# Two mixture-of-experts stages that take each slot's rows by gather and give its sums back by scatter, in a four-stage kernel

## The reference

```python
x = x + tanh(g_xattn[0]) * L0_xattn(ctx_1024, layernorm(x), ...)        # stage a
x = x + tanh(g_ffn[0])   * L0_ffn(layernorm(x), router_w, router_b, w1, w3, w2)   # stage f: 4 experts, top 2
x = x + tanh(g_xattn[1]) * L1_xattn(layernorm(x), ctx_1024, ...)        # stage g
x = x + tanh(g_ffn[1])   * L1_ffn(layernorm(x), Wg, W1, W2, W3)         # stage m: 8 experts, top 2
# an expert: y = (silu(t @ w1) * (t @ w3)) @ w2, hidden width 2048 (f) or 1024 (m)
# out = sum over the token's two experts of gate * y
```

## Time and profile before

| what | us |
|---|---|
| median of 3 runs (2413.39 to 2417.11) | 2416.28 |
| the profiled execution's own time | 2416.51 |
| its span | 2414.3 |
| TensorE busy | 1988.6 (82%) |
| TensorE weight loads busy | 1595.4 (66%) |
| VectorE busy | 1078.6 (45%) |
| ScalarE busy | 855.8 (35%) |
| GpSimd busy | 569.1 (24%) |
| stage f, 1141.7 to 1762.2 | 620.5 |
| stage g, 1762.2 to 1914.7 | 152.5 |
| stage m, 1914.7 to 2414.3 | 499.6 |

### The profile page before, as it was taken

The page is one execution under the profiler, slowest core; times in us unless marked ns, Lnnn a source line. Parts: engine busy times, 40 slices in busy tenths (PEclk is TensorE's granted clock), DMA queues, the critical chain, the costliest instruction groups (busy, mean ns, idle before and its releaser), DMA issues. The chain is left out here.

```text
span 2414.3 us, 35504 instructions
## 1 busy us (share of the span) xinstructions
PE 1988.6 (82%) x12312; PEld 1595.4 (66%) x12312; DVE 1078.6 (45%) x2301; ACT 855.8 (35%) x1799; POOL 569.1 (24%) x522
## 2 busy tenths in 40 slices
PE   3899999999999999996289999999737628888883
PEld 2577777777776777774177777777516427776772
DVE  4445454545445454433433333333254445445444
ACT  2333333433343433332333333333124234444440
POOL 2020202020202010000213333333130023445443
PEclk9999999999999999998589999999868859999896
DMA  6501010101000010000633333333560364434446
GB/s 213 182 35 47 8 39 15 40 9 34 21 32 23 10 45 8 15 8 17 217 114 100 100 100 104 103 101 99 203 215 1 110 229 138 121 122 145 133 122 179
DMA packets 114324, 214.75 MB, mean 89 GB/s; under 512 B 21584, under 2 KB 24432, under 8 KB 114188
## 3 DMA queue, kind: packets, MB, share of 16 engines
q1 hardware_dynamic: 104876, 186.02, 24.8%
q0 software_dynamic: 6144, 13.13, 1.9%
q10 hardware_dynamic: 3168, 13.89, 1.4%
HBM read 172.82 MB, written 40.17 MB: 88 GB/s over the span
## 5 line engine op out<-in xcount | busy, mean ns | idle before, releaser
L360 POOL TENSOR_TENSOR a_rows<-a_rows,a_gain_x 128x512 f32<-128x512 f32 (+1 forms) x48 | 66.2, 1379 | 773.1 <-DVE a_rows L680 773.1
L848 PE MATMUL f_banks<-f_wab_hi,f_x_hi 128*128 x448 | 185.9, 415 | 15.3 <-DVE f_wab_lo L1438 11.9
L488 PE MATMUL a_kv_ps<-a_kvin_hi,a_wk_hi 128*128 128x512 f32 (+1 forms) x512 | 196.5, 384 | 0.9 <-DVE a_kvin_lo L687 0.9
L488 PE MATMUL a_kv_ps<-a_wv_hi,a_kvin_hi 128*128 128x512 f32 (+1 forms) x448 | 185.9, 415 | 11.8 <-DVE a_k_lo L704 7.0
L848 PE MATMUL m_banks<-m_wab_hi,m_x_hi 128*128 x512 | 163.4, 319 | 31.7 <-DVE m_wab_lo L1438 28.6
L490 PE MATMUL a_kv_ps<-a_kvin_hi,a_wk_lo 128*128 128x512 f32 (+1 forms) x512 | 180.4, 352 | 0.0
L489 PE MATMUL a_kv_ps<-a_kvin_lo,a_wk_hi 128*128 128x512 f32 (+1 forms) x512 | 180.3, 352 | 0.0
L490 PE MATMUL a_kv_ps<-a_wv_hi,a_kvin_lo 128*128 128x512 f32 (+1 forms) x448 | 178.1, 397 | 0.0
L850 PE MATMUL f_banks<-f_wab_hi,f_x_lo 128*128 x448 | 177.8, 397 | 0.0
L489 PE MATMUL a_kv_ps<-a_wv_lo,a_kvin_hi 128*128 128x512 f32 (+1 forms) x448 | 177.6, 396 | 0.0
L849 PE MATMUL f_banks<-f_wab_lo,f_x_hi 128*128 x448 | 176.7, 394 | 0.0
(11 more groups left out here) (347 smaller groups left out, 4799.0 us busy)
## 6 DMA issues: line engine op xcount, KB each, us to landing
f_raw<-f_pieces SPq DMA_DIRECT2D x192, 256.0 KB, 2.8
m_raw<-m_pieces SPq DMA_DIRECT2D x192, 256.0 KB, 2.8
ahead_piece<-g_ctx ACTq DMA_DIRECT2D x4, 2880.0 KB, 37.9
a_rows<-ctx SPq DMA_DIRECT2D x8, 1280.0 KB
m_tokens<-m_zeros SPq DMA_DIRECT2D x1, 5120.0 KB, 21.0
a_wout_sb<-L_xattn_Wkv SPq DMA_DIRECT2D x8, 512.0 KB, 14.5
f_tokens<-f_zeros SPq DMA_DIRECT2D x1, 4096.0 KB
m_y_acc<-m_tokens SPq DMA_DIRECT2D x4, 1024.0 KB, 7.8
```

The lines of the kernel that those rows point to most:

```text
L360: own.link(nc.gpsimd.tensor_tensor(row, row, gain_x[0:n, :], ALU.mult))
L488: nc.tensor.matmul(out, hi_l, hi_r, start=first, stop=False)
L848: nc.tensor.matmul(out, left_hi, right_hi, start=start, stop=False)
```

## The change

In both expert stages:
- The zero writes, the scatter of tokens and the loads of `tokens` go. ScalarE's queue stores the normalised tokens to `xn`. One-hot products find, for each row of each slot, its token: VectorE builds `in_slot` (in which slot a pair lies) and `at_row` (on which row), TensorE sums 16 products of the two, and VectorE copies the result to `rows_at`. GpSimd gathers `y_acc` slot by slot, 128 rows each.
- The running sum over batches becomes shifted products with ones on TensorE; logits come out of TensorE already by token; the router is passed transposed.
- The slots' transposes and splits move into the first group, two slots ahead of `hidden`. TensorE's code is a first group of its own and a loop over the other seven, and reads the experts' registers in each.
- In group 0 GpSimd makes the low parts of `wab` (before it gathers) and VectorE those of `wy`; before it was VectorE for `wab` and GpSimd for `wy`. ScalarE splits pieces between its steps of the front. `s_sb` goes: SiLU writes `h_sb` itself.
- Each slot's sums are scattered by GpSimd after their last addition, straight to the pair's row, so that a token's two rows lie together. SyncE loads them as plain 4 KB rows; in m it has reloaded `x` by then.

In stage g the sums come in through four buffers, loaded by SyncE; ScalarE's queue starts pieces 0 and 1 at the end of f, piece 2 first thing in g, and piece 3 after the keys and values of piece 1.

```diff
 # gated_experts, SyncE
-            sp.dma_start(tokens_dram..., zeros...).then_inc(zeroed, 16)
-            sp.dma_start(y_dram[P * CORE:, :]..., zeros...).then_inc(zeroed, 16)
-            sp.wait_ge(scattered, 16 * TOP * B)
-            load_rows(0)
+            for n in range(G * PIECES):
+                load(0, n)
...
             with sp.Else():
-                sp.sem_inc(y_stored, 16)
+                sp.wait_ge(h_ready[0], CORE * G)
+                load_again()
+                sp.wait_ge(y_scattered, 16 * CORE)
...
+            for b in range(B):
+                first = 1 + TOP * M * b
+                sp.dma_start(y_got[0:M, b, :, :], y_pairs[first:first + TOP * M, :].rearrange("(m k) d -> m k d", k=TOP)).then_inc(y_loaded[b], 16)
 # GpSimd
-            for b in range(B):
-                for k in range(TOP):
-                    nc.gpsimd.indirect_dma_start(tokens_dram[:, :], ..., x_tok[0:M, b, :], None).then_inc(scattered, 16)
-            low_weights(0)
+            low_weights(0, 0, LAST)
+            pool.wait_ge(xn_stored, 32)
+            pool.wait_ge(rows_done, 1)
+            gather_rows(0)
+            low_weights(0, LAST, G * PIECES)
+            scatter_sums(0)
 # which engine makes a low part
-            return c < LAST and (g == 0 or c in SHARED)
+            return c >= LAST if g == 0 else c in SHARED
 # ScalarE, front
-            split_inner(0, 0)
-            move_tokens(0)
+            for c in range(RING):
+                split(0, 0, c)
+            deviations(0)
+            deviations(1)
+            for b in range(HB):
+                move_batch(b)
+            store_batches(0)
+            for c in range(RING, 2 * RING):
+                split(0, 0, c)
+            for b in range(HB, B):
+                move_batch(b)
+            store_batches(1)
 # TensorE
+            for i in range(B * TOP):
+                ins = nc.tensor.matmul(banks[:, CONST, 0:2 * SLOTS], at_row[0:M, i, :], in_slot[0:M, i, :, :]..., start=(i == 0), stop=(i == B * TOP - 1))
...
+            def first_group(q, turning):
+                experts = experts_of(q)
+                pe.wait_ge(wlo_pool[q], LOW0 + POOL_FIRST)
+                    turn_tokens(q, 0)
+                    turn_tokens(q, 1)
+                for s in range(size):
+                    pe.wait_ge(xlo_done[q], s + 1)
+                    hidden(q, 0, s, experts[s])
+                    if turning and s + 2 < size:
+                        turn_tokens(q, s + 2)
...
+            def other_groups(q):
+                experts = experts_of(q)
+                with pe.Fori(0, G - 1) as i:
 # VectorE, the place of a row
-                own.link(nc.vector.tensor_copy(place[0:M, :, k], pos_f[0:M, :]))
+            own.link(nc.vector.tensor_tensor(reached..., places..., slot_at..., ALU.is_ge))
+            own.link(nc.vector.tensor_tensor(in_slot[0:M, :, 0, :], reached[0:M, :, 0:SLOTS], reached[0:M, :, 1:SLOTS + 1], ALU.subtract))
+            nc.vector.tensor_tensor(at_row[0:M, :, :], row_at..., passing..., ALU.is_equal)
+            dve.wait_ge(rows_ready, 1)
+            nc.vector.tensor_copy(rows_at[:, 0, :], banks[:, CONST, 0:SLOTS]).then_inc(rows_done, 1)
```

More of the change, by code:

```diff
@@ L1020, in gated_experts @@
         raw_loaded = [both(f"raw_loaded{n}") for n in range(RING)]
-        rows_loaded = [both(f"rows_loaded{n}") for n in range(STORES)]
         st_ready, xhi_done, xlo_done = both("st_ready"), both("xhi_done"), both("xlo_done")
@@ L1102, in _, with load_again @@
+            def load_again():
+                if x_out is not None:
+                    sp.dma_start(x_res[0:M, :, :], x_in.rearrange("b p d -> p b d")).then_inc(x_again, 16)
+            for n in range(G * PIECES):
+                load(0, n)
             sp.wait_ge(expert_done, 2)
             used = sp.value_load(expert[0:1, SLOTS:SLOTS + 1], min_val=0, max_val=SLOTS)
-            for n in range(LAST, G * PIECES):
-                load(0, n)
-            for first in range(0, CORE, 4):
-                end = min(first + 4, CORE)
-                sp.wait_ge(add_done[0], ADD0 + CORE * (G - 1) + end)
-                store_sums(0, first, end)
@@ L1158, in _, with low_weights @@
-            pool.wait_ge(expert_done, 2)
-            used = pool.value_load(expert[0:1, SLOTS:SLOTS + 1], min_val=0, max_val=SLOTS)
-            def low_weights(q):
-                for n in range(G * PIECES):
+            def low_weights(q, first, end):
+                for n in range(first, end):
                     g, c = divmod(n, PIECES)
@@ L1195, in _ @@
[L1195 to L1204 removed]
+            act.wait_ge(const_done, 7)
@@ L1252, in _ @@
                 act.wait_ge(add_done[0], ADD0 + CORE * G)
-                split_inner(1, 0)
-                move_tokens(1)
+                for c in range(LAST):
+                    split(1, 0, c)
+                for s in range(TAIL):
+                    move_tokens(1, s)
                 for g in range(G):
-                    group(1, g)
+                    group(1, g, False)
                     if g + 1 < G:
@@ new lines, in _ @@
+            for b in range(B):
+                ins = nc.tensor.matmul(banks[:, COUNT, 0:E], ones[0:M, :], chosen[0:M, B + b, :], start=(b == 0), stop=(b == B - 1))
+            ins.then_inc(count_ready, 1)
+            pe.wait_ge(at_row_done, 1)
+            for i in range(B * TOP):
+                ins = nc.tensor.matmul(banks[:, CONST, 0:2 * SLOTS], at_row[0:M, i, :], in_slot[0:M, i, :, :].rearrange("p t s -> p (t s)"),
+                                       start=(i == 0), stop=(i == B * TOP - 1))
@@ L1309, in hidden, with turn_tokens @@
-            def hidden(q, g, s):
-                if s == 0:
-                    pe.wait_ge(wlo_pool[q], LOW0 + POOL_LOWS * g)
-                    pe.wait_ge(wlo_dve[q], LOW0 + LAST + len(SHARED) * g)
+            def turn_tokens(q, s):
+                pe.wait_ge(rows_loaded[FIRST[q] + s], 16)
+                if s >= 4:
+                    pe.wait_ge(xlo_done[q], s - 3)
+                for k in range(KD):
+                    ins = nc.tensor.transpose(token_bank(s)[:, P * k:P * k + P], y_acc[:, s, P * k:P * k + P], ident[:, :])
+                ins.then_inc(st_ready[q], 1)
@@ L1353, in _ @@
+            first_group(0, True)
+            other_groups(0)
             with pe.If(used > CORE):
                 pe.wait_ge(add_done[0], ADD0 + CORE * G)
-                turn_tokens(1)
+                for s in range(TAIL):
+                    turn_tokens(1, s)
                 pe.wait_ge(xlo_done[1], TAIL)
-                with pe.Fori(0, G) as g:
-                    group(1, g)
+                first_group(1, False)
+                other_groups(1)
         @block.vector
@@ L1479, in group @@
                         given = due
-            for c in range(LAST):
-                split(0, 0, c)
-            low_tokens(0)
+            low_tokens(0, 0)
+            low_tokens(0, 1)
             dve.wait_ge(expert_done, 2)
@@ L1612, in strided_attention @@
         x_loaded = [sem(f"x_loaded{n}") for n in range(B // 2)]
-        y_gathered = [sem(f"y_gathered{n}") for n in range(2)]
+        y_loaded = [sem(f"y_loaded{b}") for b in range(B)]
         const_done = sem("const_done")
```

507 lines of the change are left out of this document (262 added, 245 removed).

## The result

The changed kernel takes 2427.91 us (median of 5 runs, 2425.11 to 2430.45) against 2416.28 us; the ratio is 1.005, its 95% interval 1.0029 to 1.0071. It is slower by 0.5%. The forecast was 2398 us with a range of 2370 to 2420, so the time lies outside the range and on the other side of the kernel before. The profiled execution has a span of 2424.3 us, 10.0 more than the 2414.3 of before.

The account below looks back on a forecast made before the run. It saw TensorE nearly idle in the fronts of f and m, between f and g, and at the end. Terms -6.8 (f's front), -5 (m's front), -1.5 (between f and g), -5 (end) sum to -18.3: 2398.2 us, range 2370 to 2420.

Parts of the forecast that it names:

- -6.5 and +5: Between f and g: g starts 6.5 us earlier (ends 3 and 14), g itself +5 (+1 to +8); together -1.5.
- Logits at 28 us: Front of f: logits at 28 us after the stage's start instead of 29.8, -1.8 us.
- The running sum, +2.4: Fronts: the running sum goes, 16 counting products at 0.3 us stand where three did, +2.4 us.
- the one-hot products, 5.2: Fronts: 16 products at 0.3 us each and a copy, +5.2 us.
- VectorE's arithmetic, +1.8: Fronts: VectorE's operations on places, with `at_row` at 2.2 us, add 1.8 us together.
- VectorE beside GpSimd, 5.5 in each front: Fronts: VectorE's operations on two SBUF inputs meet GpSimd's low parts, 5.5 us taken between 0 and 10.4.
- The third rival: VectorE pays all of GpSimd's low parts, 10.4 us in each front, and wq lands at 34 us: 2411 us; chance 0.14.
- The reads, 0.55 us: TensorE's register reads before the first transposes cost 0.55 us each: 8.3 us for 15 in f, 9.4 for 17 in m.
- The rival of dear reads: TensorE's register reads cost 1.0 us each, making the kernel slower: 2426 us; chance 0.12.
- f's groups, +11.4: f's groups: transposes between the first group's products +5.4 us, register reads at the second group +6.
- m's groups, +12.4: m's groups: transposes of 14 slots beside products +7.7 us, register reads at the second group +4.7.
- the end, -5: End of the kernel: scatters follow the additions at GpSimd's pace, then plain loads, -5 us (ends 0 and -8).

Follow-up runs that it names:

- the wide form: Kernel with reads between and wq first, plus the router's product as two 400-token products turned back, as in the kernel before: 2393.2 us against 2399.6 without it.
- pieces early: Changed kernel with all four context pieces loaded at f's end, as before the change: 2413.9 us in set 1, 2425.1 us in set 4.
- set 1: Four edits of the changed kernel (reads between, reads twice, all pieces at f's end, transfers apart), run in turn on one chip with the kernel before (2413.4 us).
- set 4: Changed kernel (2425.2 us), all pieces at f's end, reads between and transfers apart, run in turn on one chip with the kernel before (2413.1 us).
- wq first: Changed kernel with ScalarE issuing the third context piece only once wq has landed, the fourth after the third's values are moved: 2411.5 us.
- set 5: Kernel with reads between, wq first and two wide router products, unaltered (2373.0 us) and with gathers held to four or six slots of lead (2376.3, 2374.8 us).

## Why the prediction was wrong

The forecast missed by 30 us against the median and 28 against the profile (-18.3 foreseen, +10.0 found). Three steps failed. The logits took 34.4 us and not 28, since the narrow products had no price. The transfers beside the products were taken to cost ScalarE and VectorE nothing, and the stalls cost 10 to 14 us in m. And g waits for wq, which came 56.5 us after f's last addition where the terms -6.5 and +5 make 53.2. By the prediction's own steps:

- **Logits at 28 us: wrong, +6.4.** I priced the change as what goes (a turn and a turn back) and asked what ScalarE and VectorE would do meanwhile, and gave the 32 narrow products no price. On TensorE turns and routing take 15.8 us, from 1161.24 to 1177.0, where the wide form and the turns took 12.6, and the first turn is 1.5 us later. The wide form gave 6.3 us back in two stages.
- **The running sum, +2.4, and the one-hot products, 5.2:** the counting took 6.3 us and the sixteen products 7.0, at 0.44 us each, not 0.3. Under-sized by some 3. The sum for m is also off by itself: 41.9 for the start and 2 us more for its tables give 57 for the rows, and it goes on with 55.5.
- **VectorE's arithmetic, +1.8:** right; `at_row` took 2.29 us for the 2.2 foreseen.
- **VectorE beside GpSimd, 5.5 in each front: over-sized.** Two operations took 0.89 and 1.35 us instead of 0.28 each: 1.7 us in f, and some 2.5 in m. The rule of the Trainium skill, "SBUF — State Buffer", "Who interferes with whom", fits the stretched rows, but few of the low parts met the chain. The third rival, which had VectorE pay 10.4 us in each front, is out by this. So the rows were known at 58.0 and 60.9 us, 5 us later than foreseen.
- **The reads, 0.55 us: 0.64.** The choice nearest to SyncE's row was right in kind; over 62 reads it is 5.6 us. With the turns of the first two slots, which run at the low clock, it puts 2.3 us on each front. The 200 ns of the Trainium skill, "Runtime: NRT & Kernel Launch", "Instruction fetch mechanics", are a third of what TensorE's reads cost here. The Trainium skill gives them there for register loads that the runtime puts in, and these are the kernel's own, from SBUF, so "which is this case" in the prediction was too much. The rival of dear reads named 2426 us, which is the time, but not its reason: at 1.0 us a read it would have had 15 us of reads in f's front, and there are 10.
- **f's groups, +11.4: right** (+10.6), with some luck: the first Silu of f is 2.8 us late too, and the same kernel's groups took 9.6 to 15.0 us more than before in the profiles of the other sets.
- **m's groups, +12.4, and the end, -5: +25.0 and -9.4.** Together that is +15.6 for +7.4. Without stalls (pieces early, set 1) the groups take 379.9 us with all reads, 6.5 more than before and less than foreseen, probably as the turns hid better, and the end 36.3, which is 4.8 less and as foreseen; so the end itself was priced rightly. With stalls m's groups last 394 to 398 us. The late additions do not matter, as the scatters keep their own pace; from m's first `hidden` to the first scatter it is 380.5 us in the changed kernel and 370.1 without the stalls, 378.1 to 380.3 in three more profiles with them. The end differs by 3.5 more, for a reason that no run shows. So the step that failed is one that is not in the text: that transfers issued beside the products are free for ScalarE and VectorE.
- **Between f and g, -6.5 and +5: both wrong, and the errors partly cancel, by luck.** Counted from f's last addition, g started 14.8 earlier and was 18.4 longer, +3.6 for the -1.5. The -6.5 was to come from two pieces moved behind the barrier; with all four ahead of it g starts about as early (12.8 us after the last addition, set 1; 16.3 in set 4, beside 13.6 of the changed kernel). The step "g gives +1 to +8" took wq 27 to 34 us after g's start; it came at 42.3. What counts is the time from f's last addition to wq: 54.7 us before, 56.5 after, 55.3 to 58.5 in the others that leave wq last and scatter beside the additions, and 40.3 with wq first. From wq to g's end it is 128.6 us for 126.8 before. wq stands behind the sums' way out, x, the sums' way in and the pieces, and moving pieces within that line moves neither wq nor, by much, g's start. Pieces early and late differ by 0.1 us side by side.

In a set without stalls the changed kernel was not run; the early-pieces kernel, its equal in set 4, took 2413.9, and so the change is worth about nothing there (estimated, by that kernel) and costs 10 to 12 us in the sets with stalls, where it ran. That 2413.9 lies inside the forecast's range: it is the stalls that carry the time out of it. Of the 28 us that the forecast missed, 15 lie in the two fronts (7.3 and 7.6), 5 between f and m, and 8 in m's groups and the end together (12.6 less 4.4).

What stays open: what holds ScalarE and VectorE up. Shown is that it goes with the set, is gone where the indirect transfers are kept apart from the products, ends for ScalarE in m when the last gather lands, and is not moved by moving ScalarE's code. Whether the length of the train matters was asked (set 5) and not answered.

## What to carry to other kernels

Price every product that a rewrite adds on TensorE by a row of the nearest shape, also a narrow one: 32 small products with tokens as weights cost more than two wide ones and a turn back. A transfer moved within a line that ends in what the next stage waits for gains nothing; ask what is last in the line, and put it first if the next stage waits for it. Register reads between products cost nothing that could be seen, before them they cost 0.64 us each. When an engine is late, ask whether the one that it feeds keeps a pace of its own: eight microseconds of late additions cost the end nothing. And before a difference between two kernels is laid to the edit, run both in turn in one set: here three programs, run again unaltered, differed by 11 to 20 us between sets while the kernel before beside them did not.

## What the runs showed of the hardware

- A register read from SBUF on TensorE's queue: 0.64 us, from 60 added reads and 38.5 us of added waits (44.8 us by the medians of set 1 would be 0.75).
- An indirect gather or scatter of 128 rows of 2 KB keeps GpSimd 0.94 to 1.02 us (the first gather of a train up to 1.13), with 0.30 us between, about the same as 100 rows did in the kernel before.
- In some sets, ScalarE and VectorE stood still for 2 to 11 us while a train of 14 to 16 indirect transfers was issued or landing; three kernels cost 20, 19 and 11 us more there, and the kernel before, whose indirect transfers stand alone, nothing (2410.6 to 2415.8 in all five).
- After its idle time in m's front TensorE works at the lower of its two levels (1.2 of 2.4 GHz) first. Around m's first `hidden` the changed kernel, with two slots turned ahead of it, is granted 0.50 from 1992 to 1996 and 0.67 in the next 4 us; the kernel before, with 64 turns ahead of it, has 1.00 for the turns from 1992 to 1996, then an idle time, and 0.66 from 2000 to 2004.
